# A graph layer's node stage with gamma, beta and bias applied by TensorE, its products a step later, its roots earlier

## What is computed

```python
h = jnp.maximum(_layernorm(x), 0.0)                       # per node
em = jnp.concatenate([h[src], h[dst]], axis=-1)
em = relu(layer_norm(em @ msg_w + msg_b, msg_g, msg_beta)) * edge_weight[:, None]
messages = segment_mean(em, dst)                          # zero for a node without edges
gate = sigmoid(h @ gate_w + gate_b)
combined = jnp.concatenate([h, messages], axis=-1)
h_new = relu(layer_norm(combined @ upd_w + upd_b, upd_g, upd_beta))
out = x + gate * h_new + (1.0 - gate) * h
```

## Time and profile before

| | |
|---|---|
| time, median of 3 runs | 1118.11 us (1116.52 to 1118.13) |
| the profiled execution's own time | 1116.92 us |
| its span | 1115.2 us |
| node stage | about 47 to 470 us, step 5 to step 97 |
| edge stage | about 477 to 1100 us |
| busy: VectorE, ScalarE, TensorE products, GpSimd | 891.9, 882.3, 759.2, 685.4 us |

### The profile page before, as it was taken

One profiled execution on the slowest core, in us unless ns is written; L12 is line 12 of the kernel. 1 busy time (PEld: TensorE's weight loads), 2 busy tenths in 40 slices (PEclk: granted clock), 3 DMA queues, 4 the chain that ended last, 5 costly groups with the idle time before them and its releaser, 6 DMA issues.

```text
span 1115.2 us, 20924 instructions
## 1 busy us (share of the span) xinstructions
PE 759.2 (68%) x3696; PEld 599.6 (54%) x3696; DVE 891.9 (80%) x3964; ACT 882.3 (79%) x3764; POOL 685.4 (61%) x602
## 2 busy tenths in 40 slices
PE   1687777878887788854766577576656766676750
PEld 1455555555555555544655466565545555665640
DVE  7799999999999999974576676677667767778781
ACT  2699999999999999976686776677677767768870
POOL 5567676666676766745456566566656655664464
PEclk9999999999999555556888778877787787788885
DMA  4145454544545444422111111111111111111110
GB/s 134 53 146 152 146 150 146 153 143 150 151 149 148 147 147 146 130 61 76 57 50 61 49 52 61 50 52 50 61 50 51 48 62 49 51 55 45 51 55 23
DMA packets 56173, 100.67 MB, mean 90 GB/s; under 512 B 13872, under 2 KB 15744, under 8 KB 56092
## 3 DMA queue, kind: packets, MB, share of 16 engines
q1 hardware_dynamic: 35766, 64.54, 16.1%
q0 software_dynamic: 18912, 34.84, 13.0%
q10 hardware_dynamic: 1414, 0.53, 0.3%
HBM read 52.34 MB, written 51.45 MB: 93 GB/s over the span
## 4 chain that ended last, share of the span: by engine, by line
DVE 40%; PE 19%; ACT 15%; issue 12%; another core or an unknown queue 8%; POOL 2%; DVEq 1%; ACTq 1%; DMA 0%; SPq 0%; POOLq 0%
DVE work L456 8%; DVE work L445 8%; DVE work L467 6%; PE pm L1142 5%; ACT junk L397 4%; PE pm L1144 4%; DVE st L348 4%; PE pt L1089 3%; DVE work L462 3%; ACT xload L390 3%; PE py L1157 3%; ACT hrow L390 3%; DVE acc L456 3%; POOL out L572 2%
## 5 line engine op out<-in xcount | busy, mean ns | idle before, releaser
L572 POOL DMA_INDIRECT out<-work,sidx x196 | 202.5, 1033 | 184.7 <-DVE work L467 133.9
L567 POOL DMA_INDIRECT ring<-in_x,src_i x196 | 236.8, 1208 | 127.4 <-issue 52.6
L567 POOL DMA_INDIRECT ring<-in_x,gidx x196 | 241.6, 1233 | 105.5 <-DVE work L445 51.7
L1089 PE MATMUL pt<-ident,hrow 128*128 128x128 f32 x588 | 139.3, 382 | 114.4 <-ACT hrow L390 98.6
L1126 PE MATMUL py<-w_u,work 128*128 128x129 f32 x784 | 203.5, 440 | 0.0
L424 ACT ACTIVATE work<-work,gt 128x128 f32<-128x128 f32 x589 | 200.9, 409 | 1.6 <-issue 1.0
L1126 PEld LDWEIGHTS py<-w_u,work 128*128 128x128 f32 x784 | 174.7, 327 | 40.4 <-issue 40.4
L1089 PEld LDWEIGHTS pt<-ident,hrow 128*128 128x128 f32 x588 | 93.5, 192 | 143.7 <-ACT hrow L390 126.8
L390 ACT ACTIVATE hrow<-xload,nb,rs 128x128 f32<-128x128 f32 x392 | 161.9, 488 | 8.3 <-issue 5.8
L456 DVE SCALAR_TENSOR_TENSOR work<-py,rs,g_upd 128x128 f32<-128x128 f32 x588 | 162.9, 336 | 5.1 <-ACT rs L377 5.1
L397 ACT ACTIVATE junk<-py 128x128 bf16<-128x128 f32 x588 | 151.9, 274 | 6.0 <-issue 3.4
(11 more groups left out here) (164 smaller groups left out, 1748.0 us busy)
## 6 DMA issues: line engine op xcount, KB each, us to landing
xload<-in_x SPq DMA_DIRECT2D x98, 256.0 KB
out<-work SPq DMA_DIRECT2D x98, 256.0 KB
running_sums<-acc SPq DMA_DIRECT2D x49, 256.0 KB
ring<-in_x,src_i POOLq DMA_INDIRECT x196
ring<-in_x,gidx POOLq DMA_INDIRECT x196
out<-work,sidx POOLq DMA_INDIRECT x196
w_all<-in_L_gnn_msg_w ACTq DMA_DIRECT2D x1, 128.0 KB
w_all<-in_L_gnn_upd_w ACTq DMA_DIRECT2D x1, 128.0 KB
```

Source lines behind the costliest of these rows:

```text
L567: pool.indirect_dma_start(out=dest, out_offset=None, in_=rows, in_offset=bass.IndirectOffsetOnAxis(ap=idx, axis=0), **(if_tail if rows is ...
L572: pool.indirect_dma_start(out=out, out_offset=bass.IndirectOffsetOnAxis(ap=idx, axis=0), in_=rows, in_offset=None, **if_tail).then_inc(s, 16)
L1089: last = nc.tensor.transpose(dest[:, k * H:(k + 1) * H], rows[:, k, :], ident[:, :])
```

## The change

- **Algebra.** gamma goes into the weights: w_n = (upd_w centred) * gamma, 128 columns. The products u = h w_n + bias * gamma stand in one PSUM bank of a group. As relu(u/std + beta) * gate = relu(u + beta * std) * gate/std, TensorE adds beta * std to u: ScalarE computes std as well (`dev`, a second exp in `rstds`), TensorE transposes the 128 x 4 std to 4 x 128 (`devt`), ScalarE copies it out (`dev_row`), and TensorE multiplies 5 rows (4 of std, one of ones for the bias) with `shifts` (5 rows of 512: beta in its group's columns, bias times gamma), the `shift` product.
- **The squares** need products without gamma, which now come from a second set of products, with w_q: 127 columns that keep the sum of squares of all 128, and the gate's as the 128th. They stand in another bank, with one bias product of 512 columns. So eight products per group instead of four.
- **VectorE** replaces gamma and beta by `rectified`, one instruction of 512 elements: max(u, 0) times gate/std (`grs`, a product of 4 elements). ScalarE's four gated relu of the node stage are gone.
- **Order.** TensorE's flips and products are one step later against the group (g+2, g+3); ScalarE's squares come in step g+4, two on either side of the roots, which now stand ahead of the evacuation; ScalarE's copy of std in step g+5, TensorE's shift and VectorE's rectify in step g+6, final in g+7. PSUM banks: four for u, two for q, one for flips, one for std.
- **Edges** begin beside node step NG + 4 (LAG), since their banks are those of the node stage.
- **Preparation** gets more: both weight sets, bias parts, six more instructions of VectorE, seven more small loads, and one more by SyncE.

```diff
+LAST_IN_PM = max(g for g in range(NG) if g % 4 == 2)
...
+ROOT = float(H) ** 0.5
+BIAS = 3 * H + 1
+LAG = 4
...
-        if beside is not None and s >= n_groups:
-            beside(Group(s - n_groups))
+        if beside is not None and s >= n_groups + lag:
+            beside(Group(s - n_groups - lag))
...
+        node_u = [banks[:, 0], banks[:, 1], pm[:, :, :], pa[:, :].rearrange("p (k h) -> p k h", h=H)]
+        node_q = [banks[:, 2], pt[:, 1, :].rearrange("p (k h) -> p k h", h=H)]
+        node_d = banks[:, 3]
...
+            if d is nd:
+                nc.scalar.activation(dev[:, s.at % 4, :], lnv[:, s.at % 4, G:2 * G], ACT.Exp, scale=0.5)
...
+        def node_post(act, g, slot, first):
+
+            q = node_q[g.at % 2]
+            if first == 0:
+                nd["upd"].after(act, g)
+            squares(q[:, first:first + 2], slot, G + first, 2, 0, width=H - 1, k0=first)
+            if first:
+                one_mark(nd["post"], act, g, nc.scalar.activation(ge[:, g.at % 2, :], q[:, :, H - 1], ACT.Exp, scale=-1.0))
+
+        def dev_row(act, g):
+
+            nd["devt"].after(act, g)
+            if beyond(g, 2):
+                nd["shift"].after(act, g.back(2))
+            one_mark(nd["dev"], act, g, nc.scalar.activation(dev_t[0:G, g.at % 2, :], node_d[0:G, 0, :], ACT.Copy))
...
+        def scaled_gate(dve, g, slot):
+
+            one_mark(nd["grs"], dve, g, nc.vector.tensor_tensor(grs[:, g.at % 4, :], gt[:, g.at % 4, :],
+                                                                rs[:, slot, G:2 * G], ALU.mult))
+
+        def rectified(dve, g):
+
+            nd["shift"].after(dve, g)
+            nd["grs"].after(dve, g)
+            one_mark(nd["t"], dve, g, nc.vector.scalar_tensor_tensor(
+                t_buf[:, g.at % 2], node_u[g.at % 4], 0.0, grs[:, g.at % 4, :].unsqueeze(2).to_broadcast([P, G, H]),
+                ALU.max, ALU.mult))
...
-                g = s.back(4)
+                g, v = s.back(4), s.back(5)
                 fin, new = live(g, NG), live(s, NG)
-                if fin:
-                    gain(dve, nd, g, 0)
+                L = nd["stats"]
                 if new:
                     dve.wait_ge(s_x[s.at % XS], s.rounds(16, 16, XS))
-                    L = nd["stats"]
-                    row_stats(L, s, xload[:, s.at % XS, 0:1], 0)
-                if fin:
-                    gain(dve, nd, g, 1)
-                if new:
-                    row_stats(L, s, xload[:, s.at % XS, 1:2], 1)
-                if fin:
-                    gain(dve, nd, g, 2)
+                    row_stats(L, s, xload[:, s.at % XS, 0:2], 0)
                 if live(s.back(1), NG):
                     minus_mean(dve, nd, s.back(1), G)
+                if live(v, NG):
+                    nd["rstd"].after(dve, s)
+                    scaled_gate(dve, v, s.at % 4)
+                f = s.back(7)
+                if live(f, NG):
+                    final(dve, nd, f, o[:, f.at % 4], t_buf[:, f.at % 2], "t")
                 if new:
                     L.begin(dve, s)
                     L.mark(row_stats(L, s, xload[:, s.at % XS, 2:4], 2))
                 if fin:
-                    if beyond(g, 4):
-                        dve.wait_ge(s_st[g.at % 4], g.rounds(16))
-                    nd["rstd"].after(dve, s)
-
-                    one_mark(nd["gamma"], dve, g, by_std(t_buf[:, g.at % 4], py[:, g.at % 2], s.at % 4, G, g_upd, ALU.mult, G,
-                                                         L.wait if new else None))
-                elif new:
+                    gain(dve, nd, g, 0)
+                if live(s.back(6), NG):
+                    rectified(dve, s.back(6))
+                if new:
                     L.wait()
+                if fin:
+                    gain(dve, nd, g, 1)
                 if new:
                     aggregate(L, s, G)
                 if fin:
+                    gain(dve, nd, g, 2)
+                    if beyond(g, 4):
+                        dve.wait_ge(s_st[g.at % 4], g.rounds(16))
                     nd["gain"].after(dve, g)
                     for k in range(G):
                         last = mix_row(g, k, hrow[:, g.at % 4], xload[:, g.at % XS], o[:, g.at % 4])
                     one_mark(nd["mix"], dve, g, last)
-                    beta(dve, nd, g, t_buf[:, g.at % 4], be_upd)
-                f = s.back(6)
-                if live(f, NG):
-                    final(dve, nc.vector, nd, f, o[:, f.at % 4])
...
-            dve.wait_ge(s_w, 11 * 16)
+            dve.wait_ge(s_w, 18 * 16)
...
-            run_steps(dve, node_step, NG, 6, 9, 8, first=4, beside=edge_step)
+            run_steps(dve, node_step, NG, 7, 9, 8, first=4, beside=edge_step, lag=LAG)
...
-                r = s.back(6)
-                if live(r, NG):
-                    gated_relu(act, nd, r, 1, done=False)
                 if live(s.back(1), NG):
                     nd["stats"].after(act, s.back(1))
-                if live(s.back(4), NG):
-                    nd["post"].after(act, s.back(4))
+                if live(s.back(5), NG):
+                    nd["post"].after(act, s.back(5))
                 logs(act, nd, s, 2 * G)
-                filling = not beyond(s, 4)
-                if filling:
-                    rstds(act, nd, s, 2 * G)
+                p = s.back(4)
+                if live(p, NG):
+                    node_post(act, p, (s.at + 1) % 4, 0)
+                rstds(act, nd, s, 2 * G)
+                if live(p, NG):
+                    node_post(act, p, (s.at + 1) % 4, 2)
                 g = s.back(2)
                 if live(g, NG):
-                    evacuate(nd, g, ht_dst[:, g.at % 4, :], pt[:, g.at % 2, :], ACT.Copy, "ht", "flip")
-                if not filling:
-                    rstds(act, nd, s, 2 * G)
-                if live(r, NG):
-                    gated_relu(act, nd, r, first=1)
+                    evacuate(nd, g, ht_dst[:, g.at % 4, :], pt[:, 0, :], ACT.Copy, "ht", "flip")
+                if live(s.back(5), NG):
+                    dev_row(act, s.back(5))
                 g = s.back(1)
                 if live(g, NG):
                     nd["nb"].after(act, g)
                     one_mark(nd["h"], act, g, h_rows(g, hrow[:, g.at % 4], xload[:, g.at % XS], 0))
-                if live(s.back(3), NG):
-                    post(act, nd, s.back(3), (s.at + 1) % 4, G)
...
+                if not beyond(s, 3):
+                    nd["grs"].after(act, Group(NG - 3 + s.at))
...
-            run_steps(act, node_step, NG, 6, 9, 8, beside=edge_step)
+            run_steps(act, node_step, NG, 5, 9, 8, beside=edge_step, lag=LAG)
...
-                g = s.back(1)
+                g = s.back(2)
                 if live(g, NG):
                     nd["h"].after(pe, g)
-                    one_mark(nd["flip"], pe, g, flip(pt[:, g.at % 2, :], hrow[:, g.at % 4]))
-                g = s.back(2)
+                    if beyond(g, 1):
+                        nd["ht"].after(pe, g.back(1))
+                    one_mark(nd["flip"], pe, g, flip(pt[:, 0, :], hrow[:, g.at % 4]))
+                v = s.back(5)
+                if live(v, NG):
+                    nd["rstd"].after(pe, s)
+                    if beyond(v, 1):
+                        nd["dev"].after(pe, v.back(1))
+                    one_mark(nd["devt"], pe, v, nc.tensor.transpose(node_d[0:G, 0, :], dev[:, s.at % 4, :], ident[:, :]))
+                v = s.back(6)
+                if live(v, NG):
+                    nd["dev"].after(pe, v)
+                    one_mark(nd["shift"], pe, v, nc.tensor.matmul(node_u[v.at % 4], dev_t[:, v.at % 2, :], rows4(shifts),
+                                                                  start=False, stop=True))
+                g = s.back(3)
                 if live(g, NG):
                     nd["ht"].after(pe, g)
+                    if beyond(g, 4):
+                        nd["t"].after(pe, g.back(4))
+                    for k in range(G):
+                        nc.tensor.matmul(node_u[g.at % 4][:, k, :], ht_dst[:, g.at % 4, k * H:(k + 1) * H], w_n,
+                                         start=k == 0, stop=False)
                     if beyond(g, 2):
-                        nd["gamma"].after(pe, g.back(2))
-                    for k in range(0, G, 2):
-                        put_bias(py[:, g.at % 2, k:k + 2, 0:H + 1], H, 2 * H + 1)
+                        nd["post"].after(pe, g.back(2))
+                    q = node_q[g.at % 2]
+                    put_bias(q, 2 * H + 1, BIAS)
                     for k in range(G):
-                        last = nc.tensor.matmul(py[:, g.at % 2, k, 0:H + 1], ht_dst[:, g.at % 4, k * H:(k + 1) * H],
-                                                w_u1[:, :], start=False, stop=k % 2 == 1)
+                        last = nc.tensor.matmul(q[:, k, :], ht_dst[:, g.at % 4, k * H:(k + 1) * H], w_q[:, :],
+                                                start=False, stop=k == G - 1)
```

(31 more changed lines are left out.)

102 lines of the change are left out of this document (64 added, 38 removed).

## The result

The changed kernel takes 1174.44 us (median of 4 runs, 1171.91 to 1180.02), the kernel before 1117.51 (4 runs, 1116.52 to 1118.13): ratio 1.052, 95% interval 1.048 to 1.056. The prediction said 1125, in a range of 1100 to 1144: slower, as it leaned, but the size lies outside its range. The profiled execution took 1174.27 us with a span of 1172.5, which is 57.3 us more than the span before.

A forecast was written before the change was run, and what follows sets the result against it. It took a ring between TensorE and ScalarE to set the node step at 4.60 us, as before the change. Profiled 1116.9 us + 0 for 92 steps + 3.5 start + 4.5 end = 1125 us, range 1100 to 1144.

The forecast's parts named there:

- the clock under the new load: TensorE in the node stage: rests 0.4 us in 4.6, so fast level (2.4 GHz) from the second or third step on.
- rival (d): Node stage: the clock drops time and again, slow steps of 7.5 us, 1145 to 1390 us in all; chance 0.07.
- What the two full engines lose: Node step: VectorE's work falls from 4.60 to 3.78 us, ScalarE's to 3.6; alone they would give a step of 3.8.
- The ring: Node step: TensorE's half 3.74, ScalarE's 0.84 and a wait of 0.02 make one turn of 4.60 us; bounds 4.30 to 4.80.
- The change-overs: TensorE in the node step: about 0.10 us for each change of weight shape, not for bf16 beside f32.
- Start: Before the steady node steps: weights' preparation 1.5 us and first steps at the slow clock 2 us, +3.5 (1 to 8).
- End: Node to edge stage: edges begin 20.1 us after the last aggregates, 13.7 later, 9 come back: +4.5 us (0 to 10).
- (b): Node step: change-overs fall away or something in the ring is shorter, 4.3 to 4.5 us, 1097 to 1115 us; chance 0.25.
- (e): Node step: the ring isn't closed and VectorE sets 3.8 us, 1051 us in all; chance 0.03.
- (c): Node step: a longer ring, 4.7 to 4.8 us and over, by waits between TensorE's groups, up to 1144 us; chance 0.18.

The follow-up runs named there:

- z1: Changed kernel with deviations and shifts over 128 rows and the roots one square later, behind three squares: 1128.05 us, ratio 1.009 to the kernel before.
- z2: Changed kernel with deviations and shifts of 32 rows, 27 of them zeros: 1140.09 us, ratio 1.019 to the kernel before.
- z3: Changed kernel with deviations and shifts of 64 rows: 1130.16 us, ratio 1.011 to the kernel before.
- x1: Changed kernel with ScalarE's roots ahead of all four squares: 966.57 us, ratio 0.953 to the kernel before.
- x3: Changed kernel with the four flips of a node step issued twice: 1037.19 us, ratio 1.021 to the kernel before.
- x4: Changed kernel with roots ahead of the squares and deviations and shifts over 128 rows: 936.6 us, ratio 0.923 to the kernel before.
- w4: Changed kernel with roots first, full rows in deviations and shifts, and a 128-row bias, on a 1014 us chip: 913.63 us, ratio 0.901 to the kernel before.
- x2: Changed kernel with deviations and shifts over 128 rows, 123 of them zeros, order unchanged: 1006.9 us, ratio 0.993 to the kernel before.
- y1: Changed kernel without edit, timed on another chip: 1074.19 us against 1014.5 for the kernel before, ratio 1.058.
- y2: Kernel before without edit, traced on the other chip: 1014.62 us.
- z4: Changed kernel with roots first, full rows in deviations and shifts, and a 128-row bias, on a 1117 us chip: 1136.19 us, ratio 1.016 to the kernel before.
- y4: Kernel before with the four transposes of a node step issued twice: 1054.18 us, ratio 1.040 to the kernel before.

## Why the prediction was wrong

The step that failed is that of **the clock under the new load**: "In the new ring at 2.4 GHz TensorE rests 0.84 less four flips of 0.11, 0.4 us in 4.6, so I take the fast level from the second or third step on." It took the level to be kept, and put the cost of losing it at nothing. The rest was measured at 0.55 in 4.80, and the fast level lasted 14 to 27 us at a time. Losing it costs 43.7 us of the 57.3, and is the prediction's rival (d), which had a chance of 0.07 (it put a slow step at 7.5 us; the 29 take 5.8 to 6.9). That rival had named the reason, 5-row weights that do not count as work: z1, z2 and z3 bear it out (0.87, 0.96 and 1.00 with 5, 32 and 64 rows in equal steps; 0.99 with 128 and a longer rest), and x1 and x3 show the other half, that with hardly a rest even 5 rows do. The prediction gave it little, although it had itself noted that no row showed such weights: the fast level that it read in the edge stage was reached with products mostly over 128 rows. That the time came out slower, as the prediction leaned, is in part luck: its sum was slower for start and end alone (+8), and these were -4.8 together.

The other parts, in its order:
- **What the two full engines lose** was right for VectorE. With the ring shortened (x4, w4) the step is 3.81, where VectorE was given 3.78; in w4's step at 200 us its aggregates are 3.78 apart. ScalarE was given 3.6, and has no idle time in that step either: its share was 0.2 too low.
- **The ring** was right in every arrow and 0.20 us short, 18.4 us in all. That 4.80 is also its upper bound is chance: the bound stood for waits between TensorE's groups, and 0.13 of the 0.20 lie in ScalarE's half, the rest in shift. The terms: shift to the next start 1.05 where 0.96 was taken (0.09; in x2 it is 0.96 with no change of rows behind it, so the stream's 0.86 was 0.10 too low); rs to transpose 0.34 where 0.27 was (0.07); dev to rs 0.09 for 0.05 and the squares 0.52 for 0.50 (0.06); the rest agrees to 0.02.
- **The change-overs** belong to the number of rows, as it assumed, and not to bf16 beside f32: x2 takes three of them away with 0.28 us. The 4-column transpose pays none (0.12 to shift in x2). The Trainium skill (TensorEngine Tiling (Array Packing), Key Properties) says that a change of tiling mode drains TensorE; here 5, 32 and 64 rows beside 128 cost 0.29 us a step alike, and 4 columns beside 128 nothing. Whether a product of fewer rows is another mode in that page's sense no run here shows.
- **Start**, +3.5 predicted, was -2.3: on the first chip the step with the edge lists' preparation took 11.0 us instead of 13.6. On the second chip the starts are 0.1 us apart (40.34 and 40.45). The preparation's added operations cost nothing that shows.
- **End**, +4.5 predicted, was -2.5: the edges begin 21.6 us after the aggregates for 20.1 predicted, but 17.8 came back instead of 9. On the second chip the part behind the last aggregates is 1.8 us longer (551.3 us in y1, 549.5 in y2), so of the 2.5 us not even the sign belongs to the change. Where the time comes back was not looked into.
- **Rivals.** (b) is excluded by the turn of 4.80 and (e) by the waits; (c) was right with its 4.80, though not with its reason, and (d) came on top of it. Both were treated as alternatives, when they add up.

Two things are open. Why the clock holds at 64 rows and not at 32 is only ordered by the runs, not explained. And whether roots first, alone or with full rows, keeps its gain on a 1117 us chip was not seen: no batch with either met one, and z4's stops may belong to the full-row bias or to any kernel as dense as that. Only z1 to z4 were timed there, and all four are slower than the kernel before, by 0.9 to 1.9%.

## What to carry to other kernels

When an engine that rests at its slow clock is to be made the bound, cost its half of the work at both levels and ask what keeps the fast one: idle time and products with few rows weighed together here. Try early to pad the contraction of small products to the full rows with zeros: at the shift product it saved 0.29 us a step and the some 40 us of lost clock, and at the bias 23 us more in an untouched stage. The latter holds for chips on which the kernel before takes 1014 us; on the one of 1117 us the kernel with it was slower than before, so time such a kernel on both. In a ring over two engines move the link that the other engine waits for (here two roots) ahead of what that engine does not need.

## What was not expected of the hardware

- In this kernel, steps with a shift of 5 rows hold TensorE's fast level only where it hardly rests: 0.87 granted with a rest of 0.55 us in 4.80, 1.00 with 0.10 (x3) or none (x1).
- A share of rest is another one at the other level. z1 rests 0.80 us in 4.81 at the fast level and keeps it. y4 rests only 0.63 in 5.16 at the slow level and stays there for up to 75 us; once it has the fast one it rests 2.03 in 4.6 (the row at 200.91 us: [2.03 <-ACT hrow L390]) and has lost it 6.8 us later.
- Chips differ in how soon a signal of TensorE arrives. The trace records the increments of a semaphore. An increment is called late here when it is recorded more than 1 us after the end of the instruction that makes it, and without a record when none comes before the same semaphore's next increment is due. TensorE's, as late / without a record / of all:
```
kernel, chip                    node stage (47 to 380 us)   edge stage (560 to 900 us)
before, 1117 us                  1 / 31 / 145               73 /  3 / 112
changed, 1117 us                 0 / 77 / 252               67 /  6 / 113
full rows (z1), 1117 us          0 / 68 / 276               79 /  3 / 115
32 rows (z2), 1117 us            2 / 94 / 268               74 /  3 / 115
full-row bias (z4), 1117 us     63 / 55 / 256               79 /  7 / 115
before, 1014 us (y2)             0 /  0 / 144                0 /  0 / 137
changed, 1014 us (y1)            0 /  0 / 253                0 /  0 / 139
full-row bias (w4), 1014 us      0 /  1 / 350                0 /  0 / 136
```
On the 1117 us chips the edge stage of every kernel has late increments, the node stage hardly any but that of z4. Records that are missing are another thing: the kernel before has 31 in its node stage and keeps its 4.60 us a step.

In the stop of z4 above, the increments of w_q, the transposes, the deviations' transpose and shift, which end between 228.99 and 230.39, are all recorded from 231.50 to 231.64. The edge stage of before has such waits too: between 700 and 1000 us 13 waits of ScalarE, 43.5 us, have no releaser that the trace names, and in y2's edge stage (640 to 940 us) none has. So part of the longer edge step on such a chip, 12.12 us for 9.83, may be these waits; how much is not shown. What holds the signals up no run here shows.
